# A state-space loop on one core: GpSimd multiplies by C in pairs of units, with drives, sums and gate moved

## What is computed

```python
xz = seq @ W_in.T;  u, z = split(xz, 2)                 # u, z: 128 channels
u  = silu(causal_conv4(u) + conv_b)
dt = softplus((u @ W_x.T)[:4] @ W_dt.T + b_dt)
Bm, Cm = ...                                            # 16 values each per time step
for t in time:                                          # 16 states s for each channel
    h[s] = exp(dt*A[s]) * h[s] + (dt*u) * Bm[s]
    y    = sum_s h[s] * Cm[s]
out = ((y + u*Dp) * silu(z)) @ W_out.T
```

## Time and profile before

| | |
|---|---|
| time, median of 3 runs | 5599.91 us (5599.64 to 5601.52) |
| profiled execution | 5600.13 us, of which the span is 5598.3 us |
| busy over the span | PE 89%, DVE 82%, ACT 62%, POOL 80% |
| the state-space loop | DVE's first drive starts at 56.05 us, its last gate at 3444.54 us |
| one chunk in it | 52.82 us |

### The profile page before, as it was taken

One profiled execution on the slowest core, in us unless ns is written; L12 is line 12 of the kernel. 1 busy time (PEld: TensorE's weight loads), 2 busy tenths in 40 slices (PEclk: granted clock), 3 DMA queues, 4 the chain that ended last, 5 costly groups with the idle time before them and its releaser, 6 DMA issues. The chain is left out here.

```text
span 5598.3 us, 68281 instructions
## 1 busy us (share of the span) xinstructions
PE 5008.4 (89%) x22742; PEld 2624.2 (47%) x22742; DVE 4589.1 (82%) x6402; ACT 3460.1 (62%) x4188; POOL 4501.3 (80%) x2067
## 2 busy tenths in 40 slices
PE   7999999999999999999999998883769999999998
PEld 3444444444444444444444444531446666666666
DVE  8999999999999999999999998103868778688665
ACT  5666676676676666666666663000557777777776
POOL 6999999999999999999999996001447777677676
PEclk9999999999999999999999999796889999999999
DMA  5656566666656565666565563394689999999999
GB/s 203 212 208 216 207 211 214 212 209 213 212 208 214 210 214 209 213 212 211 208 217 207 211 213 134 141 401 132 135 157 198 197 199 198 196 197 197 196 199 186
DMA packets 1416310, 1137.13 MB, mean 203 GB/s; under 512 B 1212667, under 2 KB 1222547, under 8 KB 1408533
## 3 DMA queue, kind: packets, MB, share of 16 engines
q1 hardware_dynamic: 1411480, 1131.52, 73.2%
q10 hardware_dynamic: 4478, 1.25, 0.2%
HBM read 814.23 MB, written 21.09 MB: 149 GB/s over the span
## 5 line engine op out<-in xcount | busy, mean ns | idle before, releaser
L822 POOL TENSOR_TENSOR mamba_state<-mamba_state,mamba_c_row 128x1024 f32<-128x1024 f32 x1024 | 2407.8, 2371 | 108.4 <-DVE mamba_state L795 98.4
L693 PE MATMUL mamba_y_ps<-mamba_state,ident 128*128 128x512 f32 x4096 | 1956.0, 602 | 146.1 <-POOL mamba_state L822 144.8
L795 DVE TENSOR_TENSOR_SCAN mamba_state<-mamba_decay,mamba_b_ps 128x1024 f32<-128x1024 f32 x704 | 1609.6, 2286 | 95.2 <-DVE mamba_b_ps L781 1.9
L1957 POOL TENSOR_TENSOR l3s_el<-l3s_s_sb,l3s_eh 128x1024 f16<-128x1024 f32 x512 | 1088.7, 2150 | 429.1 <-DMA l3s_et<-l3s_el 212.7
L693 PEld LDWEIGHTS mamba_y_ps<-mamba_state,ident 128*128 128x128 f32 x4096 | 745.1, 189 | 995.8 <-issue 660.4
L1965 DVE TENSOR_SCALAR_CACHE_REDUCE l3s_s_sb<-l3s_s_ps 128x512 f32<-128x512 f32 x1024 | 684.7, 686 | 233.6 <-PE l3s_s_ps L1898 228.8
L1912 PE MATMUL l3s_o_ps<-l3s_vt,l3s_et 128*128 128x257 f16 x4096 | 805.3, 275 | 58.8 <-DMA l3s_et<-l3s_el 26.7
L781 DVE TENSOR_TENSOR mamba_b_ps<-mamba_dtu,mamba_b_ps 128x1024 f32<-128x1024 f32 x704 | 848.9, 1206 | 1.3 <-PE mamba_b_ps L681 1.3
L1941 ACT ACTIVATE l3s_eh<-l3s_s_sb,l3s_shift 128x1024 f16<-128x1024 f32 x512 | 583.9, 1140 | 380.7 <-issue 178.0
L795 DVE TENSOR_TENSOR_SCAN mamba_state<-mamba_b_ps,mamba_b_row 128x1024 f32<-128x1024 f32 x320 | 728.9, 2278 | 103.6 <-POOL mamba_b_row L816 103.4
L771 ACT ACTIVATE mamba_decay<-mamba_dt,mamba_A 128x1016 f32<-128x1016 f32 x704 | 782.9, 1133 | 12.5 <-DVE mamba_state L795 9.4
(11 more groups left out here) (325 smaller groups left out, 5247.1 us busy)
## 6 DMA issues: line engine op xcount, KB each, us to landing
mamba_c_row<-mamba_c_rows SPq DMA_DIRECT2D x1024, 512.0 KB, 3.8
mamba_b_row<-mamba_c_rows SPq DMA_DIRECT2D x320, 512.0 KB, 4.8
l_ring_a<-in_L_conv_W SPq DMA_DIRECT2D x28, 1024.0 KB, 10.9
l2b_ring_b<-in_L_conv_W SPq DMA_DIRECT2D x26, 1024.0 KB, 10.9
l_ring_a<-in_L_conv_W SPq DMA_DIRECT2D x14, 704.0 KB, 12.7
l2b_ring_b<-in_L_conv_W SPq DMA_DIRECT2D x13, 704.0 KB, 12.7
l_ring_a<-in_L_conv_W SPq DMA_DIRECT2D x14, 640.0 KB, 12.1
l2b_ring_b<-in_L_conv_W SPq DMA_DIRECT2D x13, 640.0 KB, 12.1
```

Of the source, the lines that this page charges most:

```text
L693: last = nc.tensor.matmul(y_ps[:, half(h)], C["ident"][:, :], state[:, s % STATES, half(h)], start=False, stop=(s == S - 1))
L795: nc.vector.tensor_tensor_scan(state[:, s % STATES, :], by, add, 0.0, ALU.mult, ALU.add).then_inc(s_scan, 1)
L822: nc.gpsimd.tensor_tensor(state[:, s % STATES, :], state[:, s % STATES, :], c_row[:, s % C_ROWS, :], ALU.mult).then_inc(s_hc, 1)
L1957: nc.gpsimd.tensor_tensor(el[:, part, off:off + EXPW], s_sb[:, par, j * EXPW:(j + 1) * EXPW], eh[:, part, off:off + EXPW], ALU.subtract).t ...
```

## The change

The product takes two units (`DUO` = 2) in one operation of 128x2048, issued at even positions when the second unit's scan is done. So `state` has 6 slots in place of 4 and `decay` 3 in place of 4 (its slots are now counted by DVE units alone, `decay_slot`), C rows are freed and awaited in pairs, sums run 5 units behind in place of 3, the POOL units are 3, 6, 9, 12, 15 with drives issued three positions ahead, B rows are loaded earlier, and the gate stands at position 4, which is a DVE unit, ahead of that unit's drive.

```diff
-LAG = 3
-PAIRS, DECAYS, STATES, C_ROWS = 2, 4, 4, 4
+LAG = 5
+PAIRS, DECAYS, STATES, C_ROWS = 2, 3, 6, 4
+DUO = 2
-GATE_AT, OUT_AT, ADD_AT = 2, 14, 15
+GATE_AT, OUT_AT, ADD_AT = 4, 14, 15
-POOL_UNITS = (2, 4, 6, 8, 10)
+POOL_UNITS = (3, 6, 9, 12, 15)
-B_ROWS, DRIVE_AHEAD, B_LOAD_AHEAD = 5, 2, 2
+B_ROWS, DRIVE_AHEAD, B_LOAD_AHEAD = 5, 3, 5
...
+        def decay_slot(c, s):
+
+            return (by_dve(c, s) - 1) % DECAYS
+
+        def decay_free(c, s):
+
+            c_of, k = divmod(by_dve(c, s) - 1 - DECAYS, len(DVE_UNITS))
+            return c_of * S + DVE_UNITS[k] + 1
...
         def load_c(sp, c, par, s):
-            wait(sp, s_hc, unit + 1 - C_ROWS)
-            sp.dma_start(c_row[:, s % C_ROWS, :], c_dram[par, s].partition_broadcast(P)).then_inc(s_crow[s % C_ROWS], 16)
+            if s % DUO == 0:
+                wait(sp, s_hc, (unit - C_ROWS) // DUO + 1)
+            sp.dma_start(c_row[:, unit % C_ROWS, :],
+                         c_dram[par, s].partition_broadcast(P)).then_inc(s_crow[unit % C_ROWS // DUO], 16)
...
         def pe_sum(pe, c, par, s):
-            wait(pe, s_hc, unit + 1)
+            if s % DUO == 0:
+                wait(pe, s_hc, unit // DUO + 1)
...
         def act_unit(act, c, par, s):
-                wait(act, s_scan, unit + 1 - DECAYS)
-                to = decay[:, s % DECAYS, :]
+                wait(act, s_scan, decay_free(c, s))
+                to = decay[:, decay_slot(c, s), :]
...
         def pool_product(pool, c, par, s):
             unit = c * S + s
-            wait(pool, s_scan, unit + 1)
-            wait(pool, s_crow[s % C_ROWS], 16 * (c * S // C_ROWS + s // C_ROWS + 1))
-            nc.gpsimd.tensor_tensor(state[:, s % STATES, :], state[:, s % STATES, :], c_row[:, s % C_ROWS, :],
+            if s % DUO:
+                return
+            own, row = unit % STATES, unit % C_ROWS
+            wait(pool, s_scan, unit + DUO)
+            wait(pool, s_crow[row // DUO], 16 * DUO * (unit // C_ROWS + 1))
+            nc.gpsimd.tensor_tensor(state[:, own:own + DUO, :], state[:, own:own + DUO, :], c_row[:, row:row + DUO, :],
                                     ALU.mult).then_inc(s_hc, 1)
...
         def sp_unit(sp, c, par, s, prep):
             load_c(sp, c, par, s)
-            if s + B_LOAD_AHEAD in POOL_UNITS:
-                load_b(sp, c, par, s + B_LOAD_AHEAD)
+            for k in POOL_UNITS:
+                if s == max(0, k - B_LOAD_AHEAD):
+                    load_b(sp, c, par, k)
...
         def dve_unit(dve, c, par, s, prep):
-            dve_drive(dve, c, par, s)
             if s == GATE_AT and not is_first(c):
                 dve_gate(dve, c - 1, 1 - par)
+            dve_drive(dve, c, par, s)
             dve_scan(dve, c, par, s)
...
         def pool_unit(pool, c, par, s, prep):
-            late = behind(c, par, s, 1)
+            late = behind(c, par, s, DUO)
```

More of the change, by code:

```diff
@@ L577, in mamba_layers @@
         s_bdrive = sem(f"{tag}_pool_drive_ready")
-        s_crow = [sem(f"{tag}_c_row_loaded_{i}") for i in range(C_ROWS)]
+        s_crow = [sem(f"{tag}_c_rows_loaded_{i}") for i in range(C_ROWS // DUO)]
         s_hc = sem(f"{tag}_hc_ready")
@@ L690, in pe_sum @@
                     nc.tensor.matmul(y_ps[:, half(h)], weights(c)["diag_Dp"][:, :], u[:, par, half(h)], start=True, stop=False)
-            wait(pe, s_hc, unit + 1)
+            if s % DUO == 0:
+                wait(pe, s_hc, unit // DUO + 1)
             for h in range(2):
-                last = nc.tensor.matmul(y_ps[:, half(h)], C["ident"][:, :], state[:, s % STATES, half(h)], start=False,
+                last = nc.tensor.matmul(y_ps[:, half(h)], C["ident"][:, :], state[:, unit % STATES, half(h)], start=False,
                                         stop=(s == S - 1))
@@ L793, in dve_scan @@
                 wait(dve, s_drive, by_dve(c, s))
-                by, add = decay[:, s % DECAYS, :], b_ps[s % PAIRS][:, :]
-            nc.vector.tensor_tensor_scan(state[:, s % STATES, :], by, add, 0.0, ALU.mult, ALU.add).then_inc(s_scan, 1)
+                by, add = decay[:, decay_slot(c, s), :], b_ps[s % PAIRS][:, :]
+            nc.vector.tensor_tensor_scan(state[:, unit % STATES, :], by, add, 0.0, ALU.mult, ALU.add).then_inc(s_scan, 1)
         def dve_gate(dve, c, par):
@@ L911, in _ @@
                 sp.wait_ge(s_cw, 16 * TOTAL)
-                for i in range(C_ROWS):
-                    sp.wait_ge(s_crow[i], 16 * TOTAL * S // C_ROWS)
+                for i in range(C_ROWS // DUO):
+                    sp.wait_ge(s_crow[i], 16 * DUO * len(range(i * DUO, TOTAL * S, C_ROWS)))
                 for i in range(B_ROWS):
@@ L951, in _ @@
                 run(pool, pool_unit)
-                pool_product(pool, LAST, LAST % 2, S - 1)
+                pool_product(pool, LAST, LAST % 2, S - DUO)
 GRID = 4
```

## The result

| | before | changed |
|---|---|---|
| time, median | 5599.77 us (5597.28 to 5601.52) | 5627.08 us (5623.9 to 5633.27) |
| ratio to before | | 1.005, 95% interval 1.0035 to 1.0065 |
| span of the profiled execution | 5598.3 us | 5623.5 us |
| the loop, first drive to last gate | 56.05 to 3444.54 | 56.58 to 3465.51 |
| one turn (distance of two gates), the usual one | 52.82 | 53.06 |

The change makes the kernel 0.5% slower. Turns are read from the starts of DVE's gates, of which there are 64; "usual" is the value most turns have within 0.02.

A forecast was written before the change was run, and what follows sets the result against it. A loop over DVE and POOL, neither full, was taken to set the pace. Gate wait and PE's stretch make the turn 53.12 against 52.82; 62 x 0.30 plus ends gives +19, from 5600.1 to about 5620 us, range 5568 to 5645.

The forecast's parts named there:

- The pair product: On POOL, one 128x2048 product takes 4538 ns; a pair costs 4.49 us in place of 4.64.
- The stops for the drives go: On DVE, the stops of 0.48 and 1.12 us a chunk ahead of POOL units' scans disappear.
- The chain to the gate: POOL's products, then PE's sums: gate can start 26.28 us after the scan of unit 11, so it waits 1.98.
- Behind the gate: PE's work from the gate to the B row of unit 8 takes 14.02 us, DVE's 13.94: adds 0.08.
- The turn: One chunk of the loop takes 53.12 us, against 52.82 before: 0.30 more.
- The sum: Whole kernel: 62 chunks at +0.30 make +18.6; with first chunk, last chunk and end, total +19 us.
- +3.9: End of the kernel: last scan to gate takes 8.5 us in place of 4.6, so 3.9 more.
- PE's own earliest start of the sum of 12: On PE, when POOL does not delay it: 12.94 us after the scan of unit 11.
- the faster rival: Pair product at the rate of the 3606 ns add; PE sets the gate, turn 52.18, 5562 us; chance 0.19.
- things that were put at nothing: Decay and state slots, C and B rows: no cost; tightest C row need 7.2 us after release, landing about 6.8.
- the slower rival: No saving in the pair, +22 us more, or late C rows for units 10 and 11: 5645 us; chance 0.14.
- waits for DMA in places where I set nothing: Sign in the profile that would show the forecast wrong: DMA waits where no cost was set.

The follow-up runs named there:

- Run 7: Changed kernel with products of one unit and the old POOL units (2, 4, 6, 8, 10), drives two ahead, B rows as before: 5604.4 us, ratio 1.0001 to the kernel before.
- Run 3: Changed kernel with `dtu` made for only 32 columns from the third chunk on, so its output differs: 5543.0 us, ratio 0.9899 to the kernel before.
- run 8: Changed kernel with `dtu` at position 11 on POOL, ahead of the product of units 10 and 11: 5589.9 us, ratio 0.9981 to the kernel before.
- run 10: Changed kernel, products in pairs, with PE's last sum ahead of the B row of unit 4: 5601.1 us, ratio 0.9998 to the kernel before.
- run 1: Changed kernel with the drive of unit 4 ahead of the gate: 5618.5 us, ratio 1.0035 to the kernel before.
- runs 2: Changed kernel with products of one unit (`DUO` = 1), all other edits kept: 5537.9 us, ratio 0.989 to the kernel before.
- run 9: Changed kernel with products of one unit and PE's last sum ahead of the B row of unit 4: 5504.3 us, ratio 0.9829 to the kernel before.
- run 4: Changed kernel with the gate one position later, at position 5: 5773.7 us, ratio 1.0316 to the kernel before.

## Why the prediction was right

**The forecast held by its own steps**, 5620 against 5627.1.

- *The pair product.* Counted 4538 ns from two rows of other sizes, measured 4541. The Trainium skill's 4497 (GPSIMD Engine Reference, section 3.1) was 1% low here.
- *The stops for the drives go.* 103 us before, 6 now. Run 7 shows that the new placing of the POOL units with its earlier drives and B rows does it.
- *The chain to the gate.* From the start of the product of 10 and 11 to the sum of 12, 13.72 counted, 13.73 measured (2010.64 to 2024.37). From there to the gate 12.40 counted, 12.30 measured: the sum of 13 follows a B row, and the preparation behind it starts 1.80 later, as in the earlier trace rows (2013.69 to 2015.50), not the 1.91 that was taken. The wait was 1.98 counted, 1.85 measured. Run 3 (2.1 us taken out of POOL's part), run 8 (the same work moved inside it) and run 10 (a B row moved out of PE's part) each move the turn as this chain says, by 1.33, 0.48 and 0.46.
- *Behind the gate.* Counted 0.08 us ahead of the drive of unit 8, measured 0.09. That the stretch is as long as DVE's own way, which looked like a footnote, is what makes the gate's wait impossible to fill: run 1.
- *The turn.* 53.12 counted, 53.06 measured.
- *The sum.* Expected +19. In the profiled execution it is +25.2: 0.5 ahead of the first drive, 20.4 from there to the last gate, where the 19 was counted, and 4.2 behind the last gate (2153.8 to 2158.0), in code that the change does not touch. In the twelve profiled executions of this case that last part takes 2146.9 to 2158.1 us, so 4.2 is within its spread, and a total within 7 us of the forecast is no finer a test than that. The turns are.

Within the 20.4 the mean turn grew by 0.30, as the term had it, but that it did so exactly is luck: 0.24 is in the usual turn and 0.06 in irregular ones. The last gate waits 9.21 where it waited 4.50, +4.7 against +3.9. The last chunk has no preparation, so PE stood idle 2.89 us ahead of a B row (3444.90), and its granted clock fell; the stretch behind that row (columns as in the earlier trace rows, the granted clock is the 0.57):

```profile
3446.00:3452.00 6.00, 6.00 (x11) 2.75 (x10) 5.74 (x5) 1.21 (x2) 6.00 (x2) 0.57 0.72 233
```

The sum at 3445.92 took 3.62 us there, elsewhere 1.98. Whether the idle time is what brings the clock down was not tested. Where it did not fall in the last chunk's sums, as in run 10, the last gate waits 8.37, which is the +3.9 of the forecast.

**Where its terms were off.** PE's own earliest start of the sum of 12 was put 0.36 too late, because a wait was read as PE's work. It changed nothing in the forecast, where POOL is later still, but the faster rival's 52.18 should have been 51.73, which runs 2 and 3 reach. The faster rival did not come up: the pair has the full price of its columns.

One of the things that were put at nothing did cost something, in the place that the slower rival named. In six of the seven turns over 53.5, and in no other of the 62, POOL waits 0.56 to 1.27 us for a C row ahead of the product of units 10 and 11. The longest of them:

```profile
734.87 4.53 POOL L838 TENSOR_TENSOR mamba_state<-mamba_state,mamba_c_row 128x2048 f32<-128x2048 f32 x1 [1.23 <-DMA mamba_c_row<-mamba_c_rows]
```

Together these six turns are 4.4 us over the usual one. The seventh, 54.01, is the one with the late B row of unit 3. So the sign "waits for DMA in places where I set nothing" did show, at a price of some 5 us of 25; it does not touch the usual turn, which carries the forecast.

**Not settled.** Why the C row is late in these six chunks. A wait for a C row ahead of the product of units 0 and 1 stands in seven others (1.32 to 1.89 us) and costs nothing, as it is off the chain to the gate. The turns of 53.2 to 53.4: some hold a stop of 0.48 us ahead of a DVE unit's scan (0.13 is usual), as at unit 4 of the chunk shown above, and most versions have it at the same units; nothing in the traces names its cause.

## What to carry to other kernels

Merging two operations saves the fixed part of one (0.15 us of 4.6 here), but everything that waits for the first half then waits for both, and where the engine's queue stands on the path of a loop over several engines, that delay counts on each turn: here the turn is 1.33 us longer in pairs than singly, though they save 1.2 us of work on an engine that was not full. Follow such a loop through every engine and add up its legs, as the mean busy shares (97, 94 and 93%) tell nothing about it. Where the engine is full, as POOL is in run 9, its saved work might count; no run has pairs there without the gate waiting for them. And before an idle engine is given more work, or work is taken from a busy one, look at what that engine will wait for next: the same 1.9 us of preparation fitted into the gap ahead of one B row and cost 0.8 us a turn a few positions on.

## What the runs showed of the hardware

A POOL multiply of fp32 from SBUF cost the same per column from 1024 to 2048 columns as from 32 to 1024: 272, 2371 and 4541 ns lie on one line within 3 ns. But an add of two columns of X with 2048 results took 3606 ns, one fifth less, with 3.68 us from its start to the next one's, while DVE was busy 99% of that stage and PE not at all; why was not tried. C rows of 512 KB landed 4.8 us after issue in the changed kernel, which issues them in pairs (4.7 in runs 3 and 10), 4.2 in runs 2 and 9, which issue them singly beside the earlier B rows, and 3.8 in the kernel before and in run 7 (medians of 1024). PE's granted clock, 1.00 in the middle of the loop, fell for a stretch behind some of its idle times, and not behind others as long: in run 4 PE waits 2.67 us for the gate in the turns with a fall and in the usual ones. Where it fell, four matmuls of 512 columns took 2.5 to 3.6 us in place of 1.9 to 2.0.
